# Turned inverse started by one whole 128x1024 multiply on PoolE instead of an identity DMA and a half-width multiply, with the orders of four engines written anew

## The reference

```python
def step(S, inp):
    q_t, k_t, v_t, b_t, d_t = inp
    Sk = jnp.einsum('bhi,bhipj->bhpj', k_t, S)
    dv = b_t[..., None] * (v_t - Sk)
    upd = jnp.einsum('bhi,bhpj->bhipj', k_t, dv)
    S = S * d_t[:, :, None, :, None] + upd
    o = jnp.einsum('bhi,bhipj->bhpj', q_t, S)
    return (S, o)
...
h = _layernorm(x, axis=-1) * (1 + ca) + sa
x = x + ga * _L0_attn_ref(h, ...)
h = _layernorm(x, axis=-1) * (1 + cb) + sb
x = x + gb * _L0_ffn_ref(h, ...)
```

## Time and profile before

| what | value |
|---|---|
| runs | 1902.93, 1903.93, 1905.59 us; median 1903.93 |
| profiled execution | 1904.61 us, of which the span is 1902.9 us |
| granted clock | 0.99 (mean), 1.00 from 600 to 1500 us |
| PE busy | 1819.9 us, 96% |
| DVE busy | 1760.3 us, 93% |
| ACT busy | 1662.2 us, 87% |
| POOL busy | 1579.1 us, 83% |
| DMA | 69.89 MB, 37 GB/s in the mean |

### The profile page before, as it was taken

One profiled execution on the slowest core, in us unless ns is written; L12 is line 12 of the kernel. 1 busy time (PEld: TensorE's weight loads), 2 busy tenths in 40 slices (PEclk: granted clock), 3 DMA queues, 4 the chain that ended last, 5 costly groups with the idle time before them and its releaser, 6 DMA issues.

```text
span 1902.9 us, 64596 instructions
## 1 busy us (share of the span) xinstructions
PE 1819.9 (96%) x24518; PEld 1499.0 (79%) x24518; DVE 1760.3 (93%) x2905; ACT 1662.2 (87%) x3207; POOL 1579.1 (83%) x1403
## 2 busy tenths in 40 slices
PE   7799999999999999999999999999999999987999
PEld 6577788887788887788887778888778888876888
DVE  7899999999999999999999999999999999986987
ACT  7599999999999999999999999999999999985332
POOL 5588899888989988889988889998989998883452
PEclk9899999999999999999999999999999999998999
DMA  3111010101010110111010101001010100022000
GB/s 124 36 31 41 25 48 25 42 25 45 21 47 25 29 38 24 42 25 47 25 42 25 41 25 47 25 22 45 25 42 25 47 25 20 25 85 78 21 15 23
DMA packets 36595, 69.89 MB, mean 37 GB/s; under 512 B 7868, under 2 KB 16572, under 8 KB 33988
## 3 DMA queue, kind: packets, MB, share of 16 engines
q1 hardware_dynamic: 36292, 65.77, 11.1%
HBM read 62.86 MB, written 2.90 MB: 35 GB/s over the span
## 4 chain that ended last, share of the span: by engine, by line
POOL 54%; issue 19%; PE 15%; DVE 9%; ACT 2%; POOLq 1%; DMA 0%; DVEq 0%; SPq 0%; ACTq 0%
PE bank L729 13%; POOL e_b L563 7%; POOL kq L516 6%; POOL a_lo L578 6%; POOL pt L523 6%; POOL b_le L553 6%; POOL osc L591 5%; POOL w L508 4%; DVE ae L1936 3%; POOL a L610 3%; POOL ri L530 3%; DVE yl L1966 2%; POOL solv L625 2%; POOL solv L632 2%; PE bank L732 1%
## 5 line engine op out<-in xcount | busy, mean ns | idle before, releaser
L1911 DVE SCALAR_TENSOR_TENSOR cc<-bank,wc,cc 128x510 f32<-128x510 f32 (+2 forms) x768 | 535.9, 741 | 2.6
L729 PE MATMUL bank<-h,w 128*128 128x512 f16 (+1 forms) x1920 | 424.2, 362 | 7.3 <-POOL w L508 5.7
L729 PEld LDWEIGHTS bank<-h,w 128*128 128x128 f16 x1920 | 178.0, 99 | 144.2 <-DVE zg L2014 8.7
L516 POOL TENSOR_TENSOR kq<-cc,kq 128x1024 f16<-128x1024 f32 x64 | 137.0, 2141 | 127.1 <-ACT kq L1467 127.1
L1518 ACT ACTIVATE invT<-bank 128x512 f16<-128x512 f32 x384 | 234.8, 611 | 4.9 <-PE bank L729 4.9
L1966 DVE TENSOR_TENSOR yl<-bank,mask 128x512 f16<-128x512 f32 x320 | 218.9, 684 | 3.9 <-PE bank L729 3.9
L1513 ACT ACTIVATE inv<-bank 128x512 f16<-128x512 f32 x320 | 195.2, 610 | 11.2 <-PE bank L729 10.9
L1433 ACT ACTIVATE cc<-bank,wc 128x512 f32<-128x512 f32 x256 | 175.1, 685 | 20.8 <-PE bank L729 17.8
L729 PE MATMUL bank<-w,h 128*128 128x256 f16 x1536 | 190.9, 275 | 0.0
L729 PE MATMUL bank<-w,goT 128*128 128x256 f16 x1536 | 188.6, 273 | 0.0
L732 PE MATMUL bank<-ident,cc 128*128 128x128 f32 x1024 | 159.0, 278 | 24.0 <-ACT v L1495 22.4
(11 more groups left out here) (234 smaller groups left out, 5499.1 us busy)
## 6 DMA issues: line engine op xcount, KB each, us to landing
inv<-ident_store SPq DMA_DIRECT2D x64, 256.0 KB, 2.6
invT<-ident_store SPq DMA_DIRECT2D x64, 256.0 KB, 2.6
w_raw<-in_wh SPq DMA_DIRECT2D x15, 1032.0 KB, 5.0
out<-sol SPq DMA_DIRECT2D x16, 128.0 KB, 1.7
v<-in_x SPq DMA_DIRECT2D x3, 512.0 KB, 3.8
moving<-rank_store SPq DMA_DIRECT2D x64, 8.0 KB
standing<-rank_store SPq DMA_DIRECT2D x64, 8.0 KB
w_raw<-in_wgate SPq DMA_DIRECT2D x1, 1024.0 KB, 5.0
```

The source lines that it names most:

```text
L516: gp.tensor_tensor(kq16[:, 1].rearrange("p i t s -> p i (t s)"), cc[:, 0:2], kq16[:, 0].rearrange("p i t s -> p i (t s)"), ALU.subtract).t ...
L729: return mm(o_, l_, r_, start=start, stop=stop, skip_group_check=True)
L1911: V.scalar_tensor_tensor(dst, src, wc[:, par(s), i, 3 - j:4 - j], dst, ALU.mult, ALU.add).then_inc(sig(f"conv{i}"), 1)
```

## The change

1. The DMA of identity blocks into `invT` and its wait on SP are gone. POOL `first_inverse` now multiplies the whole 128x1024 tile (`maskT1` has ones on its diagonal, and `a1` too, so the diagonal comes out as 1) and waits for `u1_ps` in place of the DMA.
2. The orders of POOL, PE, ACT and DVE in `body` are written anew. The four DVE calls from the head of the body now stand at the end of the body before, which is the same place in the stream except in the first step.

```diff
-            def load_turned_inverse(n):
-                need(sp, "u1_ps", n - 1)
-                sp.dma_start(invT[:, n % 2], ident_store).then_inc(sig(f"it_in_{n % 2}"), 16)
...
             def first_inverse(s):
                 n = N(s)
                 need(pool, "a1", n + 1)
-                need(pool, f"it_in_{n % 2}", (n // 2 + 1) * 16)
-                gp.tensor_tensor(odds(invT[:, ring(s)]), maskT1[:].rearrange("p (b h) -> p b h", h=2)[:, :, 1].unsqueeze(1)
-                                 .broadcast_to([P, U, HP]), odds(a1[:, ring(s)]), ALU.mult).then_inc(sig("it"), 1)
+                need(pool, "u1_ps", n - 1)
+                gp.tensor_tensor(invT[:, ring(s)], maskT1[:].unsqueeze(1).broadcast_to([P, U, P]), a1[:, ring(s)],
+                                 ALU.mult).then_inc(sig("it"), 1)
```

The DVE part reads as follows, first in `first_body`, then in `body`:

```diff
...
+                decayed_queries(s0)
                 decayed_keys(s0)
                 dve.wait_ge(sig("gate_dma"), 32)
+                first_inverse(s0)
...
                 if s0:
                     convolve(1, 2, s0)
-                if s1:
-                    cross_low(s1)
-                if s0:
                     convolve(1, 3, s0)
                     if N(s0) == 1:
                         beta_columns(1, late)
...
+                    cross_low(s1)
+                if s0:
+                    squared_norms(0, s0)
+                if s1:
                     level_rows(1, s1)
-                if s0:
-                    squared_norms(0, s0)
```

PE's calls from the second values on, and behind them ACT's calls around the two middle taps:

```diff
                 if s2:
                     second_values(s2)
-                if s0:
-                    key_query(s0)
-                if s1:
+                if s1:
+                    level_right(2, s1)
                     level_left(2, s1)
-                    level_right(2, s1)
                 if s0:
                     bank_decays(0, s0, s3)
                     decay_product(0, s0)
                 if s2:
                     second_output(s2)
+                if s1:
+                    level_rows(3, s1)
                 if s0:
                     bank_decays(1, s0, s3)
                     decay_product(1, s0)
...
                 if s0:
                     squares(0, s0)
-                if s1:
-                    inverse_right(0, s1)
+                    pairs_high(s0)
                 if s2:
                     first_output(s2)
                 if s0:
-                    pairs_high(s0)
                     last_tap(2, s0)
-                    last_tap(3, s0)
                 if s1:
                     values_turned(1, s1)
+                if s0:
+                    last_tap(3, s0)
+                if s1:
+                    inverse_left(1, s1)
+                if s0:
+                    squares(1, s0)
                 if s2:
                     query_part(s2)
                     base_kept(1, s2)
```

More of the change, by code:

```diff
@@ L367, in _ @@
             for n in range(2, STEPS):
-                load_turned_inverse(n - 2)
                 load_rank(n)
@@ L669, in body @@
                     first_inverse(s1)
-                    low_half(s1)
                 if s3:
                     output_scale(s3)
-                    scaled_output(s3)
+                if s1:
+                    low_half(s1)
+                    queries_rest(s1)
                 if s0:
@@ L677, in body @@
                     rest_half(s2)
+                if s3:
+                    scaled_output(s3)
                 if s0:
                     key_norm(s0)
+                    key_columns(s0)
+                    masked_beta(s0)
                 if s1:
-                    queries_rest(s1)
                     values_half(s1)
                 if s0:
-                    key_columns(s0)
-                    masked_beta(s0)
                     decay_beta(s0)
@@ L1130, in body @@
                 if s1:
+                    key_cross(s1)
                     need(pe, 'iv', N(s1) + 1)
                     turn_values(0, s1)
-                    key_cross(s1)
                     level_left(0, s1)
@@ L1141, in body @@
                     first_values(s2)
+                if s1:
+                    level_right(0, s1)
+                    level_rows(1, s1)
                 if s0:
@@ L1157, in body @@
                     project(3, s0)
-                if s2:
-                    query_state(s2)
                 if s1:
+                    level_left(1, s1)
                     level_right(1, s1)
-                    level_left(1, s1)
                 if s0:
@@ L1166, in body @@
                 if s2:
+                    query_state(s2)
                     base_values(1, s2)
+                if s1:
+                    level_rows(2, s1)
                 if s0:
                     key_key(s0)
+                    key_query(s0)
                 if s2:
@@ L1194, in body @@
                     decay_product(1, s0)
-                if s1:
-                    level_rows(3, s1)
                 if s3:
@@ L1200, in body @@
                 if s1:
+                    level_right(3, s1)
                     level_left(3, s1)
@@ L1205, in body @@
                 if s1:
-                    level_right(3, s1)
                     level_rows(4, s1)
@@ L1670, in body @@
                 if s1:
-                    values_turned(0, s1)
                     cross_kept(s1)
                     inverse_left(0, s1)
+                    values_turned(0, s1)
                 if s2:
                     first_kept(s2)
+                if s1:
+                    inverse_right(0, s1)
                 if s0:
                     squares(0, s0)
-                if s1:
-                    inverse_right(0, s1)
+                    pairs_high(s0)
                 if s2:
@@ L1706, in body @@
                     decay_exp(0, s0)
-                    decay_exp(1, s0)
                 if s1:
                     inverse_right(2, s1)
+                if s0:
+                    decay_exp(1, s0)
                 if s2:
@@ L1713, in body @@
                     inverse_left(3, s1)
+                    inverse_right(3, s1)
                 if s0:
@@ L1716, in body @@
                 if s1:
-                    inverse_right(3, s1)
                     z_tanh(0, s1)
@@ L2162, in body @@
                     return first_body(s0)
-                if s2:
-                    z_gate(0, s2)
-                if s1:
-                    decayed_queries(s1)
-                if s2:
-                    z_gate(1, s2)
-                if s1:
-                    first_inverse(s1)
                 if s0:
@@ L2193, in body @@
                         gated(1)
-                    level_rows(1, s1)
+                    cross_low(s1)
                 if s0:
                     squared_norms(0, s0)
+                if s1:
+                    level_rows(1, s1)
                 if s2:
@@ L2244, in body @@
                     decayed_keys(s0)
+                if s1:
+                    z_gate(0, s1)
+                if s0:
+                    decayed_queries(s0)
+                if s1:
+                    z_gate(1, s1)
+                if s0:
+                    first_inverse(s0)
                 if s1 and (not s0):
```

13 lines of the change are left out of this document (removed).

## The result

The changed kernel takes 1915.53 us (median of 4 runs, 1912.39 to 1918.51) against 1903.43 us before. The ratio is 1.0062, with a 95% interval of 1.0043 to 1.0080. So it is slower by 12 us, or 0.6%. Five more runs of the same kernel beside the later experiments gave 1914.47 us and 1.0060 (1.0043 to 1.0076).

What follows compares the result with a forecast made beforehand. It took a ring of hand-overs through POOL, PE, DVE and ACT, 25.73 us a step, as the bound. Profiled 1904.6, loop 0, start +3, tail 0 gave 1907.6; being 0.7 above the median, forecast 1907 us, range 1886 to 1917.

Steps and rivals of the forecast that it cites:

- the forecast case: Whole kernel: loop ring within 0.1 us of 25.80 and start cost within its ends; 1900 to 1913 us, chance 0.50.
- the start: First two steps: decayed_keys 1.14 us later, cross_low behind the cols instructions delays project(3) and the fourth tap; +3 us (2.0 to 3.7).
- the tail: End of the kernel: only moves of under 1 us of both signs, counted as 0.
- the wait of each fourth step: PE's wait for POOL's w at each new head, about 0.37 us, 0.09 per step; was to go.
- The multiply and the DMA: POOL's wider multiply takes 1.90 us (1.28 to 2.38) and costs nothing, as POOL has room; removing the DMA gains nothing.
- The new ring: Loop path through z_tanh, ACT's groups, the fourth tap, DVE's cc to goT, and PE: 25.79, say 25.80 us a step.
- The old ring is cut: Loop ring POOL kq to a1, DVE inv to cc, ACT kq, 25.73 us, falls to 23.9 and no longer binds.
- The slower one: Rival: POOL's tail, from e_b through osq, w and a1 to DVE's inv, becomes the ring; 1917 us, chance 0.18.
- The faster rival: ACT's part of the loop is shorter than summed, so DVE's own work decides; 0.19 us less per step, 1896, chance 0.30.
- e_b's wait: Sign in the loop: POOL's e_b waits for ACT's ae as much as kq, near 0.6 us.
- the wait ahead of kq: Sign in the loop: POOL's wait ahead of kq is still there, near 0.6 us.
- the third step's zg: Sign at the start: zg of the third step comes 2 to 4 us later than before.

Runs made afterwards that it cites:

- whole_old_orders: Kernel before with only the whole 128x1024 multiply and no DMA of identity blocks into invT, all orders as before: 1904.43 us, ratio 1.0002.
- copy_ahead: Changed kernel with one unused 128x128 copy added on ACT in each step, right ahead of the fourth tap: 1928.53 us, ratio 1.0132.
- weights_wait: Changed kernel where PE's project(0) of a new head waits for two quarters of w and the first z rows for all four: 1913.63 us, ratio 1.0053.
- cross_early: Changed kernel with DVE's cross_low right behind the last cc, ahead of the cols instructions (second step) and first two gated (65th body): 1912.12 us, ratio 1.0036.
- cross_behind_old: Kernel before with whole multiply, no invT DMA, PE's w wait by halves, and the loop's cross_low behind the last cc: 1904.10 us, ratio 1.0002.
- half_new_orders: Changed kernel with the 128x512 multiply and the DMA of identity blocks of before, all orders as in the changed kernel: 1917.18 us, ratio 1.0067.
- three_edits: Changed kernel with cross_low ahead of cols and gated, PE's w wait by halves, and first-step decayed_keys ahead of decayed_queries: 1903.27 us, ratio 0.9992.
- late_in_old: Kernel before with cross_low behind the cols instructions in the second step and behind the first two gated in the 65th body: 1909.55 us, ratio 1.0029.

## Why the prediction was right and wrong

The forecast was 1907 us in a range of 1886 to 1917, with the chances split nearly evenly over faster, the same and slower. The range held the 1915.5, but the forecast case's own span, 1900 to 1913, did not. The upper end of 1917 came from a rival whose mechanism did not occur, so that it held the result is luck. Three terms were too small: the start, the tail, and the wait of each fourth step.

**The multiply and the DMA: right.** Taken at 1.90 us with 2.38 as the far end, the multiply took 2.13, between the two. It cost nothing, as whole_old_orders shows by itself. b_le's row was the wrong neighbour, which changed no sum: POOL's own work became 25.0 us a step, not 24.8. The estimate of 2.37 us, on which the floor near 1870 rests, was too high: its 2.6 cycles an element make 2.22 us at 1.2 GHz, and the remaining 0.15 has no source. Nor does one figure fit whatever is read: products of 1024 columns took 1.90, 2.13 and 2.38 us.

**The new ring: right in each term.** The path in the trace after, ACT first, then DVE, PE, and ACT one step on:

```profile
1006.41 0.60 ACT L1573 ACTIVATE zth<-bank 128x512 f32<-128x512 f32 x1 [0.59 <-PE bank L723]
...
1012.64 0.60 ACT L1528 ACTIVATE solv<-bank 128x512 f16<-128x512 f32 x1
...
1016.68 0.70 ACT L1449 ACTIVATE sq<-bank 128x512 f32<-128x512 f32 x1
...
1019.97 0.73 ACT L1424 ACTIVATE cc<-bank,wc 128x512 f32<-128x512 f32 x1
...
1032.20 0.60 ACT L1573 ACTIVATE zth<-bank 128x512 f32<-128x512 f32 x1 [0.59 <-PE bank L723]
```

```profile
1019.99 4.11 DVE L1905 SCALAR_TENSOR_TENSOR cc<-bank,wc,cc 128x510 f32<-128x510 f32 x6
...
1025.21 1.40 DVE L2015 SCALAR_TENSOR_TENSOR goT<-bank,nw_sb,goT 128x512 f16<-128x512 f32 x2
```

```profile
1026.00 0.40 PE L723 MATMUL bank<-moving,standing 72*128 72x128 f16 x4
```

z_tanh to the end of base_kept: 1013.24 - 1006.41 = 6.83 (forecast 6.83). The six groups to the end of sq: 1017.38 - 1013.24 = 4.14 (4.14). To the fourth tap's end: 1020.70 - 1017.38 = 3.32 (3.33). DVE to the first goT's end, 1025.21 + 0.75 = 1025.96: 5.26 with the hand-over (5.25). PE: decay product at 1026.00, z_tanh at 1032.20: 6.24 with the hand-over (6.24). The sum is 25.79. The six cc take 4.11 us instead of 4.01, the small wait that was foretold. Terms that go once around a steady loop add up to its step by themselves; what speaks for the path is that each agrees with its forecast, that the second cc starts 0.03 us behind the end of the fourth tap in every step, and that in copy_ahead all that is put on it comes out at the end. DVE's own path to that cc is only 0.05 to 0.1 us shorter.

**The step that failed in the loop: "PE waiting for w at each new head goes too, since POOL now arrives earlier against PE there."** It does not arrive earlier: in place of its one long wait it has two short ones ahead of e_b and osq, and w stands behind both. PE's wait was 0.37 us before and is 0.31 now, and the extra stayed at 0.29. That is 0.07 a step, 3 to 4 us in all, and weights_wait shows that it was PE's wait.

**The start: the mechanism was right, the size was not.** It was put at +3 us, from 2.0 to 3.7, and measures 5.6 to 6.0. Two terms were short. cross_low was to end at 80.5 on the clock of before. It ended at 83.86 - 2.11 = 81.75 on that clock. Most of this is the cols instructions, 5.33 us from the first to cross_low instead of 4.30: the last took 2.28 us instead of 0.35, the second 0.30 instead of 1.18. And project(3) ended 84.84 + 2.77 - 83.86 = 3.75 us behind cross_low, above the 1.8 to 3.5 that I had given it: all of it ran at a granted clock of 0.50. cross_low's place is then worth 5.0 us by cross_early's profile, and decayed_keys behind decayed_queries adds 1.14, as worked out.

**The tail: "In the tail I find moves of under 1 us of both signs" was wrong.** The same move of cross_low, here behind `gated`, costs 2.2 to 3.2 us in the last osq distance, and cross_early gets them back. I had priced `gated` at its 0.75 us of before, and did not look at what POOL runs beside it after the change.

**"The old ring is cut": right, but it was not the only one of its length.** After the change kq starts 0.7 to 0.9 us behind the end of cc, no longer 0.08, so that ring does not bind any more. The reading took no account of what stands ahead of kq on ACT itself, 0.03 us shorter, and cross_behind_old shows that taking cross_low out of the ring gains nothing by itself. The forecast did not suffer, since a step with the new orders is as long as the new ring and this had been summed for itself.

**The rivals.** The slower one gave 1917 by POOL's tail. The time is close to it, the mechanism is not. half_new_orders says nothing on it, since the rival's path ends at a1 and the multiply stands behind a1. The trace does: inv starts 0.57 us behind a1's end in the usual step and now waits for it a little, but DVE still reaches the second cc ahead of the fourth tap. Of the 0.34 us of room that the forecast left to POOL's tail, under 0.1 is left, and it does not decide. The faster rival fell with the ring's measured length. Of what was to show each step, e_b's wait came near its size (0.68 us for about 0.6), the wait ahead of kq is not there any more (1.4 us in 35 steps, not 0.6 in each), and the third step's zg came 4.8 us later, with the 2.1 us taken off by which this execution was late from the set-up on, and not 2 to 4.

## What to carry to other kernels

Price a change of order in the first and last bodies by themselves: instructions that exist in one body only stand in the same queue, and an instruction that others wait for must not get behind them. A start 0.1 us behind another engine's end may be a wait or a coincidence, and one step doesn't tell: set it beside the line ahead of it on its own engine, and see over many steps which of the two distances stays the same. A ring can be real and its cut still gain nothing, when the next path is 0.03 us shorter. When a call is moved, ask who waits for the calls that it moves past, and when a semaphore counts parts, wait for the parts that are read.

## What the hardware showed that was not expected

**DVE and POOL can block each other, and each shows it as its own length.** Of the cols instructions of the second step, the first tensor_scalar was slow with the old orders (1.18 us before), the last or the one in the middle with the new ones (2.28 after, 2.47 in half_new_orders), and each ended 0.2 to 0.4 us behind POOL's kq. After the change the last of them ran from 80.01 to 82.29, POOL's kq from 79.83 to 82.07; it takes 0.35 us in three_edits, where POOL is idle then. The two `gated` of the tail ran from 1712.01 to 1715.71, over the ends of POOL's a_lo at 1713.16 and pt at 1715.42. With the old orders it depends on where POOL's go falls: in whole_old_orders go ended at 1705.80, beside the first `gated`, and the two took 1.39 us instead of 0.75. In late_in_old the second `gated` was ahead of go by 0.02 us, and go took the extra 0.25. For the cols in late_in_old, DVE and POOL:

```profile
78.15 1.85 DVE L1877 TENSOR_SCALAR cols<-cols 128x384 f32<-128x384 f32 x1
```

```profile
77.66 2.12 POOL L516 TENSOR_TENSOR kq<-cc,kq 128x1024 f16<-128x1024 f32 x1 [4.63 <-ACT kq L1467]
```

Its end, 80.00, lies 0.22 us behind POOL's, 79.78, as it does after the change (82.29 and 82.07). No wait is printed for any of them. The Trainium skill ("SBUF — State Buffer", section "Who interferes with whom") says that DVE and GpSimd share one pair of SBUF ports as an exclusive lock. By the same section of the Trainium skill, a DVE instruction in a 2-port mode contends with GpSimd, and one with two SBUF inputs contends with a GpSimd instruction that reads SBUF. For the 2-port mode the Trainium skill adds that whoever issues first holds the pair for the whole instruction. The traces agree, with these ends and both ways round, for the long instructions; no row shows which mode the tensor_scalar ran in. Beside POOL's osc, 1.67 us for 8 columns, a `gated` kept its 0.42 us (late_in_old, 1706.23, osc's end at 1706.51), so not every POOL instruction blocks to its end.

**Executions of one kernel differ by 4 us before the first step.** The same small matmuls of PE's set-up, 26 to 38 us, in the two profiles of the changed kernel (durations in ns, smallest, median, largest, then first and last start), first the execution with the longer set-up:

```profile
L723 PE MATMUL bank<-b_le,y_acc x48: 311/421/421, 27.9 to 37.8; 128*128 128x64 f32 x48
```

```profile
L723 PE MATMUL bank<-b_le,y_acc x43: 275/275/323, 25.8 to 31.3; 128*128 128x64 f32 x43
```

Most of these matmuls took 421 or 275 ns each, although the granted clock reads 1.00 from 26 to 38 us in both, and DVE's first cc started at 48.39 or 43.56. Twelve of fourteen profiles, of both orders, show the 421. A single pair of profiles can thus not tell 4 us, and the stages must be measured from a row behind the set-up. Why a given execution gets the one or the other was not tried.
